# Hash experts of the last layer in three groups of tiles (4, 3, 1) instead of two (4, 4), with the second group ahead of the last tile's sample

## Time and profile before

| | us |
|---|---|
| median of 3 runs | 5491.76 |
| lowest, highest | 5488.08, 5493.57 |
| the profiled execution, its own time | 5489.93 |
| its span | 5487.9 |
| PE busy in it | 4087.6 |
| DVE busy | 3530.4 |
| ACT busy | 2637.4 |
| POOL busy | 774.5 |
| POOL on the gathers of L3473 | 619.7 |

### The profile page before, as it was taken

The page is one execution under the profiler, slowest core; times in us unless marked ns, Lnnn a source line. Parts: engine busy times, 40 slices in busy tenths (PEclk is TensorE's granted clock), DMA queues, the critical chain, the costliest instruction groups (busy, mean ns, idle before and its releaser), DMA issues. The chain is left out here.

```text
span 5487.9 us, 98350 instructions
## 1 busy us (share of the span) xinstructions
PE 4087.6 (74%) x37515; PEld 1540.9 (28%) x37515; DVE 3530.4 (64%) x9620; ACT 2637.4 (48%) x3507; POOL 774.5 (14%) x990
## 2 busy tenths in 40 slices
PE   4956899954799999999864999999978675601214
PEld 2333344432222222222342222222225443300002
DVE  5544666667898888898246888888843566631213
ACT  2522566642266666666513888888871021100001
POOL 0000000002000000000003000000000004777772
PEclk9967999977699999999976999999989887855557
DMA  0031000052311112011005111211110500000000
GB/s 14 1 83 22 12 12 12 5 201 85 121 22 34 31 32 82 22 34 29 8 4 169 31 42 42 45 43 41 41 17 22 159 0 9 14 13 13 13 13 8
DMA packets 141953, 219.45 MB, mean 40 GB/s; under 512 B 52533, under 2 KB 106900, under 8 KB 139354
## 3 DMA queue, kind: packets, MB, share of 16 engines
q1 hardware_dynamic: 96994, 184.66, 12.2%
q0 software_dynamic: 20480, 10.53, 1.3%
q10 hardware_dynamic: 24008, 17.98, 1.1%
HBM read 160.78 MB, written 52.28 MB: 39 GB/s over the span
## 5 line engine op out<-in xcount | busy, mean ns | idle before, releaser
L1770 ACT ACTIVATE probs<-ps 128x1024 f32<-128x1024 f32 x1632 | 1593.0, 1024 | 442.5 <-PE ps L1710 437.4
L1825 DVE CUSTOM_DVE_ANT_0 junk<-ps,mask 128x512 bf16<-128x512 f32 (+1 forms) x1664 | 1039.2, 669 | 125.6 <-PE ps L1664 87.5
L1726 PE MATMUL ps<-probs,vstack 128*18 128x512 f32 x6528 | 875.9, 600 | 0.0
L1664 PE MATMUL ps<-kturned,qturned 49*64 49x512 bf16 (+3 forms) x5178 | 790.7, 391 | 57.1 <-DVE maxima L1825 21.7
L1825 DVE CUSTOM_DVE_ANT_0 junk<-ps,nothing 128x512 bf16<-128x512 f32 (+1 forms) x1080 | 670.0, 657 | 130.5 <-PE ps L1664 130.4
L3473 POOL DMA_INDIRECT line<-table,index x640 | 619.7, 968 | 661.6 <-DVE index L3846 466.9
L1710 PE MATMUL ps<-qturned,kturned 53*64 53x512 bf16 x6528 | 625.2, 394 | 21.0 <-ACT probs L1770 13.6
L1664 PEld LDWEIGHTS ps<-kturned,qturned 49*64 49x64 bf16 (+1 forms) x5178 | 216.7, 103 | 876.1 <-issue 411.2
L3600 PE MATMUL ps<-ident,attended 128*128 128x128 f32 x8 | 3.8, 474 | 512.3 <-DVE attended L3870 512.3
L1695 PE MATMUL ps<-maskT,split 64*128 64x512 bf16 x1632 | 321.3, 384 | 2.6 <-DVE maxima L1825 2.5
L1710 PEld LDWEIGHTS ps<-qturned,kturned 53*64 53x64 bf16 x6528 | 186.4, 104 | 413.8 <-issue 253.7
(11 more groups left out here) (735 smaller groups left out, 5276.5 us busy)
## 6 DMA issues: line engine op xcount, KB each, us to landing
vstack<-values_heads SPq DMA_DIRECT2D x128, 229.5 KB, 4.6
mask_raw<-in_mask_BxSxS_if SPq DMA_DIRECT2D x8, 3202.0 KB, 18.2
kturned<-keys_parts SPq DMA_DIRECT2D x384, 54.0 KB
kturned<-keys_parts SPq DMA_DIRECT2D x384, 48.0 KB
table<-lines SPq DMA_DIRECT2D x51, 256.0 KB
line<-table,index POOLq DMA_INDIRECT x640, 2.3
keys_parts<-parts SPq DMA_DIRECT2D x24, 384.0 KB, 2.7
kapart<-keys_apart SPq DMA_DIRECT2D x160, 48.0 KB
```

The costliest lines, as they stand in the source:

```text
L1664: last = nc.tensor.matmul(ring(e)[part, 0:hi - lo], qturned[rows, h % 3, m * P + part.start:m * P + part.stop], src, start=True, stop=True ...
L1726: last = nc.tensor.matmul(k.ps[at:at + PAIR, 4, :], vstack[:, h % 2, first, t, :], probs[:, (h * KT + t) % slots, first, :], start=(t < 2) ...
L1770: nc.scalar.activation(probs[:, u % slots].rearrange("p b n -> p (b n)"), k.ps[:, bank:bank + 2, :].rearrange("p b n -> p (b n)"), ACT.Exp ...
L1825: nc.vector.tensor_tensor_reduce(junk[:, bank_of[e], 0:hi - lo], ring(e)[:, 0:hi - lo], lost, 1.0, -3.0e38, ALU.subtract, ALU.max, maxima[ ...
```

## The change

`GROUPS` gives each group's first tile and width: (0, 4), (4, 3), (7, 1). The list becomes: both chains; post 0 to 3; group 0 with post 4, 5, 6 behind experts 1, 3, 5; finish 0; group 1 (tiles 4, 5, 6), whole; post 7; group 2 (tile 7), whole. Every operation of a group works on the group's width only. Nothing else changes: not POOL's program, not the arithmetic. The core of the diff; the edits left out put the same slices into the remaining operations of `gated`, `prepare` and `centre`.

```diff
@@ -3253,6 +3253,7 @@
 HASHED, HASH_F = 8, 512
+GROUPS = ((0, 4), (4, 3), (7, 1))
 NEAR = 5
...
@@ def last_steps():
     out = [("chain", c) for c in range(CHUNKS_OF_T)] + [("post", t) for t in range(CHUNK)]
-    for half in range(CHUNKS_OF_T):
+    for half in range(len(GROUPS)):
         out.append(("prepare", half))
         for e in range(HASHED):
             out.append(("expert", (half, e)))
-            if half == 0 and e % 2 == 1:
+            if half == 0 and e in (1, 3, 5):
                 out.append(("post", CHUNK + e // 2))
         out.append(("finish", half))
+        if half == 1:
+            out.append(("post", NT - 1))
     return out
...
@@ PE
             def down(half, e):
+                width = GROUPS[half][1]
+                wide = width * P
...
-                    last = nc.tensor.matmul(k.ps[:, 6 + e % 2, :], hw2[:, e, c, :], hidden[e % 2][c], start=(c == 0),
+                    last = nc.tensor.matmul(k.ps[:, 6 + e % 2, 0:wide], hw2[:, e, c, :], hidden[e % 2][c][:, 0:wide], start=(c == 0),
...
-                turn_tiles(4, hb).then_inc(tensor_done, 1)
+                turn_tiles(4, hb, width).then_inc(tensor_done, 1)
...
-                    nc.tensor.matmul(k.ps[:, c, :], hw1[:, e, c * P:(c + 1) * P], hTc[:], start=True, stop=True).then_inc(tensor_done, 1)
+                    nc.tensor.matmul(k.ps[:, c, 0:wide], hw1[:, e, c * P:(c + 1) * P], hTc[:, 0:wide], start=True, stop=True).then_inc(tensor_done, 1)
...
-                    for j in range(CHUNK):
+                    for j in range(width):
                         last = nc.tensor.matmul(k.ps[:, 4, j * P:(j + 1) * P], bucket_wide[:, j, :], k.ident[:], start=True, stop=True)
...
@@ ACT
             def prepare(half):
-                root(dev, var, by_dve("var5", half))
+                width = GROUPS[half][1]
+                root(dev[:, 0:width], var[:, 0:width], by_dve("var5", half))
...
-                    nc.scalar.activation(hidden[e % 2][c], k.ps[:, c, :], ACT.Relu, bias=hb1[:, e, c:c + 1]).then_inc(scalar_done, 1)
+                    nc.scalar.activation(hidden[e % 2][c][:, 0:wide], k.ps[:, c, 0:wide], ACT.Relu, bias=hb1[:, e, c:c + 1]).then_inc(scalar_done, 1)
...
@@ DVE
             def prepare(half):
-                mine = [k.x[:, CHUNK * half + j, :] for j in range(CHUNK)]
-                centre(mine, hb, stats, both, var, dev, inv, by_act("dev5", half), CHUNK).then_inc(vector_done, 1)
+                first, width = GROUPS[half]
+                wide = width * P
+                mine = [k.x[:, first + j, :] for j in range(width)]
+                centre(mine, hb, stats, both, var, dev, inv, by_act("dev5", half), width).then_inc(vector_done, 1)
...
             def finish(half):
+                first, width = GROUPS[half]
+                wide = width * P
                 gated(half, HASHED - 1)
-                ts = slice(CHUNK * half, CHUNK * half + CHUNK)
+                ts = slice(first, first + width)
                 dve.wait_ge(tensor_done, by_pe("accT", half))
-                o.step(nc.vector.tensor_tensor(k.x[:, ts, :], k.x[:, ts, :], pair(k.ps[:, 4, :]), ALU.add))
+                o.step(nc.vector.tensor_tensor(k.x[:, ts, :], k.x[:, ts, :], pair(k.ps[:, 4, 0:wide]), ALU.add))
```

More of the change, by code:

```diff
@@ L3632, in finish @@
             def finish(half):
+                width = GROUPS[half][1]
+                wide = width * P
                 down(half, HASHED - 1)
                 pe.wait_ge(vector_done, by_dve("acc", half))
-                turn_tiles(4, mixed[:].rearrange("p (t n) -> p t n", n=P)).then_inc(tensor_done, 1)
+                turn_tiles(4, mixed[:].rearrange("p (t n) -> p t n", n=P), width).then_inc(tensor_done, 1)
             pe.wait_ge(counted, 1)
@@ L3654, in root @@
                 act.wait_ge(vector_done, at)
-                nc.scalar.activation(dst[:], src[:], ACT.Sqrt).then_inc(scalar_done, 1)
+                nc.scalar.activation(dst, src, ACT.Sqrt).then_inc(scalar_done, 1)
             def chain(c):
-                root(dev, var, by_dve("var", c))
+                root(dev[:], var[:], by_dve("var", c))
                 for i in range(LAYERS):
-                    root(dev, var, by_dve("var1", c, i))
+                    root(dev[:], var[:], by_dve("var1", c, i))
                     act.wait_ge(tensor_done, by_pe("v", c, i))
@@ L3686, in prepare @@
             def prepare(half):
-                root(dev, var, by_dve("var5", half))
+                width = GROUPS[half][1]
+                root(dev[:, 0:width], var[:, 0:width], by_dve("var5", half))
             def expert(half, e):
+                wide = GROUPS[half][1] * P
                 for c in range(HASH_F // P):
@@ L3719, in centre @@
                     o.step(nc.vector.bn_aggr(both[:, j, :], stats[:, j, :]))
-                nc.vector.tensor_scalar(var[:], both[:, :, 1], 1e-5, None, ALU.add).then_inc(vector_done, 1)
+                nc.vector.tensor_scalar(var[:, 0:width], both[:, 0:width, 1], 1e-5, None, ALU.add).then_inc(vector_done, 1)
                 dve.wait_ge(scalar_done, at)
-                o.step(nc.vector.reciprocal(inv[:], dev[:]))
+                o.step(nc.vector.reciprocal(inv[:, 0:width], dev[:, 0:width]))
                 for j in range(width - 1):
@@ L3879, in prepare @@
             def prepare(half):
-                mine = [k.x[:, CHUNK * half + j, :] for j in range(CHUNK)]
-                centre(mine, hb, stats, both, var, dev, inv, by_act("dev5", half), CHUNK).then_inc(vector_done, 1)
+                first, width = GROUPS[half]
+                wide = width * P
+                mine = [k.x[:, first + j, :] for j in range(width)]
+                centre(mine, hb, stats, both, var, dev, inv, by_act("dev5", half), width).then_inc(vector_done, 1)
                 dve.wait_ge(tensor_done, by_pe("hT5", half))
-                nc.vector.tensor_copy(hTc[:], k.ps[:, 4, :]).then_inc(vector_done, 1)
+                nc.vector.tensor_copy(hTc[:, 0:wide], k.ps[:, 4, 0:wide]).then_inc(vector_done, 1)
                 dve.wait_ge(vector_done, by_dve("h5", half))
-                u, v, w, sign = (hash_small[:, j, :] for j in range(4))
-                o.step(nc.vector.tensor_tensor(u, hb[:, :, 0], hb[:, :, 1], ALU.add))
+                u, v, w, sign = (hash_small[:, j, 0:width] for j in range(4))
+                o.step(nc.vector.tensor_tensor(u, hb[:, 0:width, 0], hb[:, 0:width, 1], ALU.add))
                 o.step(nc.vector.tensor_scalar(sign, u, 0.0, None, ALU.is_ge))
@@ L3905, in gated @@
             def gated(half, e):
-                o.step(nc.vector.tensor_scalar(qv[:, e % 2, :], bucketT[:], float(e), None, ALU.is_equal))
-                o.step(nc.vector.tensor_tensor(yT[:], qv[:, 0, :], qv[:, 1, :], ALU.add))
+                first, width = GROUPS[half]
+                wide = width * P
+                o.step(nc.vector.tensor_scalar(qv[:, e % 2, 0:wide], bucketT[:, 0:wide], float(e), None, ALU.is_equal))
+                o.step(nc.vector.tensor_tensor(yT[:, 0:wide], qv[:, 0, 0:wide], qv[:, 1, 0:wide], ALU.add))
                 dve.wait_ge(tensor_done, by_pe("narrow", half, e))
-                nc.vector.scalar_tensor_tensor(out=gated_out[:], in0=k.ps[:, 6 + e % 2, :], scalar=hb2[:, e:e + 1], in1=yT[:],
+                nc.vector.scalar_tensor_tensor(out=gated_out[:, 0:wide], in0=k.ps[:, 6 + e % 2, 0:wide], scalar=hb2[:, e:e + 1], in1=yT[:, 0:wide],
                                                op0=ALU.add, op1=ALU.mult).then_inc(vector_done, 1)
@@ L3912, in gated @@
                 if e == 0:
-                    o.step(nc.vector.tensor_scalar(mixed[:], gated_out[:], 0.5, None, ALU.mult))
+                    o.step(nc.vector.tensor_scalar(mixed[:, 0:wide], gated_out[:, 0:wide], 0.5, None, ALU.mult))
                 else:
-                    last = nc.vector.scalar_tensor_tensor(out=mixed[:], in0=gated_out[:], scalar=0.5, in1=mixed[:], op0=ALU.mult, op1=ALU.add)
+                    last = nc.vector.scalar_tensor_tensor(out=mixed[:, 0:wide], in0=gated_out[:, 0:wide], scalar=0.5, in1=mixed[:, 0:wide], op0=ALU.mult, op1=ALU.add)
                     if e < HASHED - 1:
```

13 lines of the change are left out of this document (7 added, 6 removed).

## The result

| | us |
|---|---|
| kernel before, median of 4 runs | 5489.92 (5484.11 to 5493.57) |
| changed kernel, median of 4 runs | 5444.88 (5435.46 to 5446.45) |
| ratio, with its 95% interval | 0.9915 (0.9898 to 0.9933) |
| span of the profiled execution | 5441.8 (before 5487.9) |

The time falls by 45 us, 0.85%; 5442 was predicted. The two spans lie 46.1 us apart.

What follows compares the result with a forecast made beforehand. Bound by POOL's gathers with idle engines, then group 1's experts behind them. After post(7), 2.5 + 3.1 + 16.2 + 1.5 = 23.3, plus 2.5 for later gathers: 25.8 instead of 75.5, so 5491.76 - 49.7 = 5442; range 5435 to 5457.

Steps and rivals of the forecast that it cites:

- Two serial pieces: Last stage before the change: gathers with idle engines up to 5395.47, then all of group 1's experts behind them.
- group 1 fits under the gathers: Three-tile group 1 ends at 5379, before tile 7's data at 5395.47; 16 us to spare, no cost on the path.
- Gathers later by 2.5 us: POOL's queue: DVE work moved beside the gathers delays them, some 0.33 us per gated, 2.5 us in all.
- rival C: Full exclusion: every shared DVE operation holds POOL for its own length, 16 us instead of 2.5; 5456, chance 0.06.
- Preparation 2.5 us: Preparing the one-tile last group behind post(7) takes 2.5 us, against 6.27 for four tiles.
- First widen and buckets 3.1: Last group: first widen hides beside bucket arithmetic of 2.7 us; with one 0.43 us matmul for turned buckets, 3.1.
- 60 matmuls 16.2 us: Last group's expert matmuls on PE, 128 columns: 4.5 us at low clock, then 11.7 at high clock.
- Rival B: PE's clock stays at 1.2 GHz in the last group: matmuls 25.8 us instead of 16.2; 5452, chance 0.18.
- Tail 1.5 us: End of the last group, after its matmuls: 3.03 us before, 1.5 with one tile.
- Rival E: A wait keeps group 1 behind post(7): 74.1 us instead of 75.5 follow, 5490, no change; chance 0.02.
- The lower end of the main case: Fastest main-case time, 5435: no gather delay, clock up at once, and 3.7 us from the fastest run before.

Runs made afterwards that it cites:

- split_only: Changed kernel's three groups, but tile 7's sample back inside group 0 as in the kernel before: 5498.43 us against 5492.05 before, ratio 1.0011.
- long_one: Changed kernel plus twelve 128x1024 DVE operations, one input in PSUM and one in SBUF, ahead of tile 7's sample; executed once, 5436.57 us.
- warm: Changed kernel plus 22 idle PE matmuls in tile 7's post and 8 ahead of the last group's transpose: 5440.74 us, last part 36.07.
- long_two: Changed kernel plus ten 128x1280 DVE operations with two SBUF inputs ahead of tile 7's sample; executed once, 5439.80 us.
- the second: The unedited changed kernel measured once more beside the kernel before on one chip: 5444.04 us against 5494.69, ratio 0.9908.
- warm_all: Changed kernel with idle matmuls in every PE gap from tile 7's sample to the first expert: 5441.7 us, ratio to before 0.9897.

## Why the prediction was right, step by step

- **Two serial pieces, and group 1 fits under the gathers**: right. Group 1 took 51.7 us with its preparation (50.8 predicted) and left 18.5 us idle (16, with the later gathers 18.5, predicted). Run split_only is the proof: the same groups in the old order lose all of the gain and 7 us more.
- **Gathers later by 2.5 us**: 2.3 measured between the samples of tiles 6 and 7, and the same 2.3 as the sum of ten gathers held beside the moved work. That the size came out so close is in part luck: with the moved work unchanged the same distance was 103.0 us in long_one and 104.1 in warm, where other gathers met other operations, 0.6 and 1.7 us more than before instead of 2.3. The size was taken from two rows with 512 columns; the mechanism was open there and is settled now. It is a price for what is under way when a gather begins. The page SBUF — State Buffer of the Trainium skill, section Who interferes with whom, names VectorE instructions in a 2-port mode and those with two SBUF inputs (these only against a GpSimd instruction that reads SBUF) as the ones that contend with GpSimd, and calls the pair of ports that the two share an exclusive lock, held by whichever issues first for its whole instruction. The traces agree that two SBUF inputs hold gathers (long_two) and that one beside an input in PSUM does not (long_one); whether the masks run in a 2-port mode no run shows. They do not agree that whichever comes first shuts the other out: a DVE operation does so to a gather, for what is left of it, but the gather at 5195.73, 0.01 us ahead of a product of 1.49 us, lengthened it by 0.02 us only. A price of the operation's whole length for every shared operation, which was rival C, does not come: a gather was held for 1.3 us at most, and only some were.
- **Preparation 2.5 us**: 5416.41 - 5413.94 = 2.47. **First widen and buckets 3.1**: 5419.62 - 5416.41 = 3.2.
- **60 matmuls 16.2 us**: 5419.62 to 5435.75, 16.1. The low clock lasted longer than I took: from 5419.62 to about 5425, some 5.4 us, where 4.5 were assumed, but the warm matmul took 0.223 us in place of 0.236. Two small errors cancel, and the low stretch is no constant: in the seven traces with this last group it is 3.2 to 5.4 us long, and the 60 matmuls take 15.1 to 16.1. Rival B did not come: the clock rose. A shade of it is real, as run warm shows: it falls in a short wait as well.
- **Tail 1.5 us**: mis-sized. It took 5437.66 - 5435.75 = 1.9. I had halved 3.03; the hand-offs between PE and DVE in it do not shrink with the width.
- **Rival E's time** was worked out wrongly: it left out the 8.4 us of group 0 that also follow post(7). Split_only shows what it would give, 88.37 + 7.2 = 95.6 us for the last part, slower than before and not equal.
- **The lower end of the main case**, 5435, was summed wrongly too: 5442 less 2.5 (no gather delay), 2.0 (16.2 - 14.2 for the clock) and 3.7 gives 5433.8. Nothing else used it.

In sum 49.7 us predicted, 49.4 measured in this stage, and the medians differ by 45.0 in the first comparison and by 50.65 in the second. The 3 us between the median and the forecast are no step of the argument: medians of the same kernel before lie between 5489.92 and 5494.69, and the first gather's start moves by more than that from trace to trace.

## What to carry to other kernels

When the end of a kernel waits for one slow queue and dense work follows it, order the work by what it needs from that queue: put everything that needs only earlier data ahead, and leave the smallest group behind, even if the division costs 7 us in itself. Price the group that is left from rows of the right width and at the clock that PE has after its pause. Where the slow queue is POOL issuing gathers, keep DVE operations that work from SBUF alone short beside it, above all those with two inputs.

## What the runs showed of the hardware

- A gather (0.945 us) that begins while a DVE operation with two SBUF inputs is under way takes the rest of that operation longer, less 0.13 us (0.09 us behind the start of one of 0.56: 1.28 us; at 5293.22 in the kernel before, 0.12 us behind one of 1.49: 2.20). Masks with one input, from SBUF to SBUF, hold it likewise (1.18 at 5203.88). One that begins 0.01 us ahead of a product pays nothing, and the product grows by 0.02 only (1.51 for 1.49). The same 15 to 17 us of DVE work cost 2.7 us in operations of 1.49 us, about 0.4 in operations of 0.33, and 0 with one input in PSUM.
- So the price of one sample was 0.7 or 1.8 us by 0.01 us of phase between POOL and DVE, and the starts of the samples moved by up to 1.7 us without any edit.
- The pause of PE at which the high clock ends need not be long: in run warm the granted clock was at 2.4 GHz from 5400.1 and fell to 1.2 GHz at 5410.4, in a wait of 1.47 us. From 5404.5 to 5410.3 PE had been busy for 3.89 us of 5.8. With idle matmuls in this gap and in the shorter ones, in warm_all, it stayed up. Whether the wait alone brought it down, or the short ones ahead of it as well, was not told apart.
